# A matrix's row in three bf16 parts, and the output's residual added by VectorE, in a two-block gated decoder

## What is computed

```python
x = x + tanh(g_xattn[0]) * L0_xattn(layernorm(x), ctx, ctx)   # 16 heads, top 90% of the keys kept
x = x + tanh(g_ffn[0])   * L0_ffn(layernorm(x))               # FP4 blocks of 16, 256 -> 704 -> 256
x = x + tanh(g_xattn[1]) * L1_xattn(ctx, layernorm(x))        # layer_norm(att + decoder_seq)
x = x + tanh(g_ffn[1])   * L1_ffn(layernorm(x))               # int8 per token, 256 -> 256
# L1_xattn has no softmax: kv = einsum('bthd,bthe->bhde', k, v); att = einsum('bqhd,bhde->bqhe', q, kv) / 4
# shapes: x, ctx (8, 512, 256) f32
```

## Time and profile before

| | us |
|---|---|
| median of 3 runs | 1346.02 (1345.36 to 1349.61) |
| the profiled execution, its own time | 1342.49 |
| its span, first to last instruction | 1340.8 |
| PE busy, all stages | 1079.4 (81%) |
| DVE busy | 1037.0 (77%) |
| ACT busy | 878.0 (65%) |
| POOL busy | 95.0 (7%) |
| mean granted clock of PE, of full speed | 0.936 |

### The profile page before, as it was taken

How to read it: one execution, slowest core, us unless ns; L and a number is a source line. 1 busy time by engine, 2 the same in 40 slices (tenths; PEclk the granted TensorE clock), 3 DMA queues, 4 the chain that set the end, 5 groups by cost and what they waited for, 6 DMA issues and landing times.

```text
span 1340.8 us, 17609 instructions
## 1 busy us (share of the span) xinstructions
PE 1079.4 (81%) x5736; PEld 514.1 (38%) x5736; DVE 1037.0 (77%) x2097; ACT 878.0 (65%) x1912; POOL 95.0 (7%) x75
## 2 busy tenths in 40 slices
PE   3999994777777677777767775888999999999986
PEld 3667673011111111111111111236666666666663
DVE  3765673798888888888888884447988888888865
ACT  2232322778999999999999993664455545554543
POOL 0010023000000000000000000001111110101012
PEclk8999997557999999999999997788999999999998
DMA  7444432011221121112222201101111111110000
GB/s 229 142 165 154 149 131 64 15 32 33 42 41 33 38 41 36 27 36 39 41 41 41 41 18 47 38 9 47 52 36 37 63 44 36 36 63 28 20 21 32
DMA packets 77776, 74.89 MB, mean 56 GB/s; under 512 B 13682, under 2 KB 71284, under 8 KB 77684
## 3 DMA queue, kind: packets, MB, share of 16 engines
q1 hardware_dynamic: 77684, 73.76, 20.2%
HBM read 44.90 MB, written 28.31 MB: 55 GB/s over the span
## 4 chain that ended last, share of the span: by engine, by line
PE 36%; ACT 33%; issue 7%; DVE 5%; SPq 1%; DMA 1%; POOL 0%; ACTq 0%; DVEq 0%
ACT ea L1061 19%; ACT prob L1069 13%; PE ps_a L1275 12%; PE ps_b L1234 6%; PE ps_c L1234 4%; PE ps_v L1234 2%; PE ps_a L1255 2%; PE ps_c L918 2%; DVE nmax L962 2%; PE ps_a L1284 2%; PE ps_v L1341 1%; PE ps_c L1367 1%; PE ps_b L1330 1%; PE ps_v L933 1%; PE ps_b L891 1%
## 5 line engine op out<-in xcount | busy, mean ns | idle before, releaser
L1061 ACT ACTIVATE ea<-ps_a,nmax 128x512 f32<-128x512 f32 x512 | 361.3, 744 | 31.9 <-DVE nmax L962 31.8
L962 DVE TENSOR_REDUCE nmax<-ps_a 128x2 f32<-128x1024 f32 x256 | 312.8, 1223 | 70.0 <-PE ps_a L891 68.5
L1069 ACT ACTIVATE prob<-ps_b 128x1024 f32<-128x1024 f32 x256 | 278.2, 1087 | 46.2 <-PE ps_b L891 46.2
L891 PE MATMUL ps_b<-q_st,k_st 52*128 52x512 f16 x512 | 102.2, 395 | 143.1 <-ACT prob L1069 139.5
L891 PEld LDWEIGHTS ps_b<-q_st,k_st 52*128 52x128 f16 x512 | 25.1, 93 | 368.8 <-ACT prob L1069 337.1
L1275 PE MATMUL ps_a<-wgu,xT 128*128 128x352 f32 x512 | 164.0, 465 | 2.4 <-ACT xT L1400 2.4
L918 PE MATMUL ps_c<-ea,rz 128*32 128x512 f32 x1024 | 153.7, 676 | 1.1 <-DVE rank L1005 1.1
L933 PE MATMUL ps_v<-prob,v_in 128*16 128x512 f32 x1024 | 137.2, 608 | 11.7 <-DVE att L1029 11.5
L1061 ACT ACTIVATION_READ_ACCUMULATOR ea<-ps_a,nmax 128x1 f32 x512 | 134.4, 262 | 0.0
L891 PE MATMUL ps_a<-k_st,q_st 48*128 48x512 f16 x512 | 108.0, 419 | 31.2 <-ACT ea L1061 18.4
L1275 PEld LDWEIGHTS ps_a<-wgu,xT 128*128 128x128 f32 x512 | 94.3, 191 | 49.4 <-issue 3.9
(11 more groups left out here) (233 smaller groups left out, 1614.7 us busy)
## 6 DMA issues: line engine op xcount, KB each, us to landing
q_scr<-q_p SPq DMA_DIRECT2D x24, 256.0 KB, 2.5
k_scr<-k_p SPq DMA_DIRECT2D x24, 256.0 KB, 2.5
q_st<-q_scr SPq DMA_DIRECT2D x32, 192.0 KB, 4.6
k_st<-k_scr SPq DMA_DIRECT2D x32, 192.0 KB, 4.8
mat<-m_scr SPq DMA_DIRECT2D x16, 384.0 KB, 3.0
x_in<-in_x SPq DMA_DIRECT2D x8, 512.0 KB, 5.6
c_in<-in_ctx SPq DMA_DIRECT2D x8, 512.0 KB, 4.1
v_scr<-v_s SPq DMA_DIRECT2D x8, 512.0 KB, 2.6
```

The source lines that it names most:

```text
L891: return e.matmul(bank, left[b][o:o + rows, r, t * P:t * P + P], right[b][o:o + rows, r], start=True, stop=True)
L962: e.tensor_reduce(nmax[u % 2][:, t].rearrange("p (h r) -> p r h", h=2)[:, r], ps_a[:, z % 2 * 2:z % 2 * 2 + 2], AX_X, ALU.max, negate=True ...
L1061: e.activation(ea[c % RING][:, g % 4], ps_a[:, g % 4], ACT.Exp, bias=nmax[u % 2][:, t, n:n + 1], accum_out=tot[u % 2][:, t, n:n + 1]).then ...
L1069: e.activation(prob[g % RING][:, 2 * (z % 2):2 * (z % 2) + 2], ps_b[:, :, :], ACT.Exp).then_inc(s_prob, 1)
```

## The change

1. The row of the second attention's matrix is kept apart from the matrix. DVE writes it to one partition (`r_s`), GpSimd takes it into three bf16 parts whose sum it is (`row_parts`: three casts and two subtractions of 1x256 for each batch, each waiting for the one before), SP stores them with a DMA of its own to `scr.r`, and in `feed` a second small DMA loads them as 3 x 256 bf16. The fp32 matmul with K=1 becomes a bf16 matmul with K=3.
2. `o_b` is written by DVE as `w_ps + r4` (new `output(u)`), not by ACT as a copy. The identity matmul of `r4` is left out on PE. `output` stands behind `x_round`; in the turns 17 to 20, in which no unit enters, it is one turn later, behind `q8` of the next unit.
3. ACT's `z` stands one `leave` earlier.
4. GpSimd's and DVE's work for `rs_a` is left out in turn 20, for `rs_b` in turns 19 and 20; nobody reads those values.
5. In `project`, GpSimd's `split` is cut in three calls. `split(0)` stands ahead of the first `row_parts`, `split(1)` and `split(2)` behind the seventh.

```diff
@@ project, sync @@
                 e.dma_start(scr.m[b], m_s[b % 2][:, :]).then_inc(s_out_m[b % 2], 16)
+                e.wait_ge(s_pool_r, b + 1)
+                e.dma_start(scr.r[b].unsqueeze(0), r_p[b % 2][:, :, :]).then_inc(s_out_m[b % 2], 16)
@@ project, vector: matrix_m @@
                 if b >= 2:
-                    e.wait_ge(s_out_m[p], 16 * (b // 2))
-                e.tensor_scalar(m_s[p][:, DC * D:], psE[:, 1, 0:D], mean[p][:, DC:], None, ALU.add).then_inc(s_dve_m, 1)
+                    e.wait_ge(s_out_m[p], 32 * (b // 2))
+                if b >= 2:
+                    e.wait_ge(s_pool_r, b - 1)
+                e.tensor_scalar(r_s[p][:, 0], psE[0:1, 1, 0:D], mean[p][0:1, DC:], None, ALU.add).then_inc(s_dve_m, 1)
@@ project, gpsimd @@
-            fp4.split(e)
+            po = Tally(s_pool)
+
+            def row_parts(b):
+
+                x, y = r_s[b % 2], r_p[b % 2]
+                e.wait_ge(s_dve_m, b + 1)
+                if b >= 2:
+                    e.wait_ge(s_out_m[b % 2], 32 * (b // 2))
+                for n in range(2):
+                    e.tensor_copy(y[:, n], x[:, n]).then_inc(*po.up())
+                    e.wait_ge(*po.now())
+                    e.tensor_tensor(x[:, n + 1], x[:, n], y[:, n], ALU.subtract).then_inc(*po.up())
+                    e.wait_ge(*po.now())
+                e.tensor_copy(y[:, 2], x[:, 2]).then_inc(s_pool_r, 1)
+
+            fp4.clear(e)
+            fp4.split(e, 0)
+            for b in range(B - 1):
+                row_parts(b)
+            for k in range(1, 3):
+                fp4.split(e, k)
+            row_parts(B - 1)
@@ feed, sync: turn @@
                 e.dma_start(mat[u1 % 2][:, :], scr.m[u1 // 2]).then_inc(s_ldm[u1 % 2], 16)
+                e.dma_start(mat_row[u1 % 2][:, :], scr.r[u1 // 2]).then_inc(s_ldm[u1 % 2], 16)
@@ feed, gpsimd @@
-        for i in range(TURNS):
+        for i in range(TURNS_A):
...
-            e.wait_ge(s_ve_b, i + 1)
-            e.tensor_tensor(rs_b[p][:, :, :], ve_b[p][:, :, :], half[:, :, :], ALU.pow).then_inc(s_rs_b, 1)
+            if i < TURNS_B:
+                e.wait_ge(s_ve_b, i + 1)
+                e.tensor_tensor(rs_b[p][:, :, :], ve_b[p][:, :, :], half[:, :, :], ALU.pow).then_inc(s_rs_b, 1)
@@ feed, tensor: turn @@
-                e.matmul(y_ps.rearrange("p (n d) -> p n d", n=N), one_row[:, :],
-                         mat[p][0:1, DC * D:].unsqueeze(1).to_broadcast([1, N, D]), start=True, stop=False)
+                e.matmul(y_ps.rearrange("p (n d) -> p n d", n=N), ones16[0:3, :],
+                         mat_row[p][:, :].unsqueeze(1).to_broadcast([3, N, D]), start=True, stop=False)
...
                 e.wait_ge(s_dve_r1, min(i + 2, UNITS))
-                e.wait_ge(s_act_out, u4)
-                e.matmul(w_ps, ident[:, :], flat(r4[u4 % 3][:, :, :]), start=True, stop=False)
-                bias_row(w_ps, 1)
+                e.wait_ge(s_dve_out, u4)
+                bias_row(w_ps, 1, first=True)
@@ feed, scalar: turn @@
-            if u5 is not None:
-                e.wait_ge(s_pe_last, u5 + 1)
...
-                e.activation(flat(o_b[u5 % 2][:, :, :]), w_ps, ACT.Copy).then_inc(s_act_out, 1)
             if u0 is not None:
                 x_T(u0)
-                for q in range(4):
+                for q in range(3):
                     leave(u0, q)
...
             if u0 is not None:
+                leave(u0, 3)
                 leave(u0, 4)
@@ feed, vector @@
+        def output(u):
+            e.wait_ge(s_pe_last, u + 1)
+            if u >= 2:
+                e.wait_ge(s_sto[u % 2], 16 * (u // 2))
+            e.tensor_tensor(flat(o_b[u % 2][:, :, :]), w_ps, flat(r4[u % 3][:, :, :]), ALU.add).then_inc(s_dve_out, 1)
+
         def turn(i):
...
                 ins.then_inc(s_dve_q, 1)
+                if i > UNITS:
+                    output(u5 - 1)
+                if u5 == UNITS - 1:
+                    output(u5)
...
             if u0 is not None:
                 x_round(u0)
-            variances_b(i)
+            if u0 is not None and u5 is not None:
+                output(u5)
+            if i < TURNS_B:
+                variances_b(i)
```

More of the change, by code:

```diff
@@ L354, in round, with clear, split @@
         e.tensor_tensor(q, q, mag, ALU.add).then_inc(self.s_round, 1)
[L356 to L357 removed]
+    def clear(self, e):
         for n in (FC - 1, 2 * FC - 1):
             e.memset(self.gn[:, n], 0.0).then_inc(self.s_zero, 1)
[L360 to L368 removed]
+    def split(self, e, k):
+        po = self.pool
+        _, y, n, nb = self.third(k)
+        q, mag, grid = self.temps(k, nb)
+        e.wait_ge(self.s_round, k + 1)
+        if k:
+            e.wait_ge(self.s_split, k)
+        e.tensor_tensor(grid, q, mag, ALU.subtract).then_inc(*po.up())
+        e.wait_ge(*po.now())
+        e.tensor_tensor(y, grid, spread(self.sc[:, n:n + nb], nb), ALU.mult).then_inc(self.s_split, 1)
     def free(self, e, n):
@@ L451, in project @@
         s_dve_mean = m.sem("dve_mean")
+        s_pool, s_pool_r = m.sem("proj_pool"), m.sem("pool_r")
         s_act_ln, s_act_rs = m.sem("act_ln"), m.sem("act_rs")
```

62 lines of the change are left out of this document (27 added, 35 removed).

## The result

The changed kernel takes 1330.61 us (median of five runs, 1329.81 to 1333.29), the kernel before 1346.02 in the same session: a ratio of 0.9884, with a 95% interval of 0.9868 to 0.9901. Run once more later it took 1330.72, a ratio of 0.9886 (0.9869 to 0.9902). The forecast was 1328.0 with a range of 1321 to 1336: the sign and the size are right, the centre 2.6 us too low. The profiled run of the changed kernel is the slowest of its five (1333.29, span 1331.6), and the profiled execution of the kernel before (1342.49) is faster than any of its five timed ones, so the two traces alone are only 9.2 us apart.

What follows compares the result with a forecast made beforehand. PE sets the turn of `feed`, 27.10 us, forecast to become 25.41. `feed` gains 21.3 us and `project` loses 3.6: -17.7, so 1328.3 against the median of 1346.02, predicted as 1328; range of 8 in 10: 1321 to 1336.

Steps and rivals of the forecast that it cites:

- The bf16 row at 0.22: PE in `feed`: a bf16 row takes 0.22 us instead of the fp32 row's 1.06, saving 0.84 a turn.
- DVE's round, 25.0 to 25.1: DVE in `feed`: its round without idle time, `output` added, is 25.0 to 25.1 us, some 0.3 below PE's turn.
- Turns 4 to 14: `feed`: turn 4 gains 1.80 us, turns 5 to 14 gain 1.69 each, 16.9.
- Turn 15 and the last ones: End of `feed`: turn 15 gains 1.80 us; turns 16 and 17 gain the row's 0.84 once.
- The unread refinements, 0 to 0.24: Last int8 rounding in `feed`: leaving out the roots ahead of it gives 0.24 us at most, counted as 0.
- The end of `project`, +2.6: `split(1)` and `split(2)` behind batch 6's row parts end at 216.6, delaying PE's weight transposes 2.6 us (+1.0 to +5.0).
- DVE in the roundings, +1.0: `project`: row parts slow DVE's `round(1)` and `round(2)`, PE losing 0.9 and 0.4; 0.3 returns from `kvs`: +1.0 us.
- my second rival: `project`: every row part in both roundings takes its full length from DVE; `project` loses 6.5 us, time 1331; chance 0.09.
- DVE as the bound: `feed`: a hand-over or lost overlap costs DVE 0.8 us more, turn 25.9, time about 1334; chance 0.14.
- GpSimd hidden: `project`: row parts at 1.5 us and no blocking, `project` loses 0.7, time 1325; chance 0.09.
- Slower than before: `project`: one batch's row parts take over 22 us and eat the 21.3 gained; chance 0.04 with anything else slower.
- The row that gets no cheaper: `feed`: what follows the row waits for `decT` anyhow; 0.84 a turn lost, time 1340; chance 0.04 with other partial gains.

Runs made afterwards that it cites:

- the two halves: Each against the kernel before: the matrix row in bf16 parts alone, 1338.66 us; all the rest of the change without that row, 1336.89 us.
- the two added instructions: The changed kernel with two more 128x512 additions on DVE, read by nothing, behind `output` in turns 5 to 15: 1338.82 us.
- the runs with parts of 10.2 us: 16 more casts in each batch's row parts: in the changed kernel 1337.89 us; with `split(1)`, `split(2)` ahead of row parts of batches 4, 5, 1331.84.
- the later kernels: The changed kernel with `split(1)`, `split(2)` ahead of row parts of batches 5, 6: 1327.34 us; 4, 5: 1326.53; that with a `kvs(5)` wait: 1324.65, again 1327.50.

## Why the prediction was right, step by step

- **PE sets the turn.** Right. PE is busy for all but 0.39 us, and the two halves alone gave 26.37 and 26.25, against 26.35 and 26.25 worked out from the same rows.
- **The bf16 row at 0.22.** Mis-sized. Its pitch is 0.31 (1092.53 to 1092.84), so it saves 0.75 and not 0.84. That is the whole difference between 25.41 and 25.51. The price was taken from a bias row, whose neighbours are others. PE's weight loads (PEld in the timeline of the same turn) show the difference:

```profile
1092.84 1.59 PEld L1265 LDWEIGHTS ps_v<-mat,decT 128*128 128x128 f32 x8 [0.23 <-issue]
...
1101.41 1.71 PEld L1265 LDWEIGHTS ps_c<-w,q8T 128*128 128x128 f32 x8
```

Behind the bias row the next product's load starts together with the row (1101.41), behind the new row it starts 0.31 later, with the product itself. The kernel before has the same, 1099.76 behind its bias row and 1090.22 behind the fp32 row of 1089.17, so it could have been read there. Why the load comes later is not shown.
- **The identity matmul, -0.96, and output on DVE, +0.11.** Right: 26.25 from 27.10 in the half that holds only these, and a gap of 0.39 where I had said about 0.4.
- **DVE's round, 25.0 to 25.1.** Right: 24.97 by the idle time, 24.9 by the two added instructions. "About 2 us ahead of `o_b`" in the list of signs was wrong, and contradicts this step: a round of 25.0 in a turn of 25.5 leaves 0.5, and 0.54 is there. The 2 us would have been those of the first such turn only (0.99 there).
- **Turns 2 and 3 gain nothing.** Right. Turn 3 takes 23.32 us, before 23.35, and `x_T` at its end stood for `xg` in PE's timeline:

```profile
976.31 0.66 PE L1286 MATMUL ps_a<-ident,xg 128*128 128x128 f32 x4 [0.63 <-DVE xg L1621]
```

- **Turns 4 to 14.** 1.80 and ten of 1.69, 18.7, were forecast; 1.69 and ten of 1.59, 17.6, came. The term that was off is the row's pitch alone.
- **Turn 15 and the last ones.** Wrong. 2.64 forecast, 1.3 came, and all of the 1.3 is the unread refinements (next point): with them put back the stretch takes 76.5 us as before. Up to the first transposes of the last hidden values, where I had 1.80, the trace shows 0.36 (29.81 to 29.45). The row gives 0.73 there (29.08 in the kernel with it alone). The identity matmul of turn 15 stands behind the down product in PE's order, off the chain, so its 0.96 should not have been counted. And `z` ahead of the fourth `leave` costs 0.4 in that turn. Behind it the 0.36 is lost again (46.7 us before, 47.1 with the refinements back), and the 0.84 of turns 16 and 17 doesn't show. PE's granted clock is lower in this stretch, 0.86 against 0.91 from `x_T` of turn 15 to the end, and the last but one group of eight products takes 3.61 us instead of 2.00. The sum had no term for the clock; how much of the loss is the clock's was not measured by itself.
- **The unread refinements, 0 to 0.24.** Mis-sized: 1.3 us by the trace. I had read what stands between ACT's `n4` and the last rounding in the kernel before. That is 0.24. But in the new order `output` of the unit before, 0.6 us, stands ahead of them on the same engine, so they end 0.84 after `n4` does. I had named that 0.6 and used it as a reason to count nothing, where it pushes the roots onto the chain. And DVE's leftovers outlast the store for 0.6 more.
- **GpSimd's parts, 3.1 us a batch.** Right: 2.85 us (93.42 to 96.27), with 0.39 to 0.46 for a cast and 0.66 for a subtraction.
- **The end of `project`, +2.6.** The path was right, a stretch was missing. GpSimd's last third was forecast for 216.6, which is 146.6 after batch 0's store, and ended at 146.5. What I missed is that DVE's `m_mean` is held until then, so that 1.04 us of `r_s`, `m_s` and the hand-over come behind it and not beside it: 3.5 in the profiled pair, 1.7 against a `project` whose clock falls.
- **DVE in the roundings, +1.0.** Wrong: nothing in sum. The two engines did meet, and GpSimd paid (timeline of all engines, changed kernel; the row parts are batch 4's, beside `round(1)` at the start of batch 6):

```profile
160.56 2.25 POOL L771 CAST r_p<-r_s 1x256 bf16<-1x256 f32 x1 [19.45 <-DVE r_s L668]
...
160.81 1.74 DVE L349 TENSOR_TENSOR fq<-gn,fs 128x1536 f32<-128x1536 f32 x1
...
162.59 1.04 DVE L351 TENSOR_SCALAR fm<-fq 128x1536 uint32<-128x1536 uint32 x1
...
162.89 1.25 POOL L773 TENSOR_TENSOR r_s<-r_s,r_p 1x256 f32<-1x256 f32 x1
...
163.66 1.30 DVE L353 TENSOR_SCALAR fm<-fm 128x1536 f32<-128x1536 f32 x1
...
164.21 1.01 POOL L771 CAST r_p<-r_s 1x256 bf16<-1x256 f32 x1
...
165.00 1.83 DVE L355 TENSOR_TENSOR fq<-fq,fm 128x1536 f32<-128x1536 f32 x1
...
165.30 2.06 POOL L773 TENSOR_TENSOR r_s<-r_s,r_p 1x256 f32<-1x256 f32 x1
...
167.54 0.41 DVE L639 SCALAR_TENSOR_TENSOR rb<-rows,psE 128x256 f32<-128x256 f32 x1
```

The parts took 7.25 us here instead of 2.85; the rounding's four instructions took 1.74, 1.04, 1.30 and 1.83 instead of 1.75, 0.96, 0.96 and 1.76, so 0.5 us together, inside the room of 0.58 that the earlier trace rows showed. PE's next product (L532, now L538) was on time, 6.98 us after the start of its `gram` products in both traces. `round(2)` looks the same (DVE 1.60, 0.98, 1.24 and 1.70 us instead of 1.61, 0.89, 0.89 and 1.62). The 0.3 that I gave back for the free `kvs` came: from batch 4's store to batch 5's it is 22.24 us instead of 22.48. But batches 3 and 4 each come 0.1 later in every kernel with row parts, for a reason that isn't traced, so batch 6's store stands 133.2 us after batch 0's in both traces. (The `kvs` rows of 0.42 and 1.53 us in the earlier trace rows are those of batches 6 and 5; I had called them 7 and 6.) The Trainium skill, "SBUF — State Buffer", section "Who interferes with whom", has the second to issue wait for the first. `kvs` behind GpSimd's long multiplication agrees (1.53 us, ending 0.27 after it); `m_mean`, which has one input in SBUF, was held too (1.13 us, ending 0.01 after GpSimd's). The roundings don't agree: GpSimd's first cast starts at 160.56, ahead of DVE's `fq` at 160.81, and yet `fq` takes its usual 1.74 us and the cast 2.25 instead of 0.46. Taken as a price for DVE, as in my second rival, the rule would have cost 3.9 in the two roundings; the trace has 0.5 us more work on DVE in each and no time lost.
- **SP, 0.** Right for parts of 2.85 us (`c_in` issued at 86.7, read at about 97), and the runs with parts of 10.2 us show the price beyond it: PE stood 0.93 us for a load in batch 1.

**The rivals.** DVE as the bound (1334) didn't come, by 0.5 us a turn, and the run with 1.46 us more shows what it would look like. GpSimd in DVE's way (1331.2) is nearer to the measured time than the forecast, for the wrong reason: nothing in the roundings, all at the end. GpSimd hidden (1325) is what the order of the later kernels nearly reaches, 1324.7 to 1327.5. Slower than before needed 22 us a batch; 10.2 cost 7 us. The row that gets no cheaper fell with the half that has it alone, 7.5 us less than before.

By its own steps the forecast promised 1.1 too much in the steady turns and 1.3 in the last ones, and its two terms for `project` missed in opposite directions: 3.6 forecast, 3.5 by the trace. -17.7 becomes -15.4, and 1346.0 less that is 1330.6. That `project` came out right is luck: two terms missed and cancelled. The agreement to a tenth is luck too: the 3.5 is from a kernel before whose clock stayed up, with 1.7 the sum would be -17.2, and the interval of the measured ratio allows 13.3 to 17.8 us. What the prediction had right for its own reason is the steady turns, 17.6 of 18.7.

## What to carry to other kernels

Once the pitch of a turn is known to be one engine's, compare the new turn with every other engine's round, its idle time taken out; the difference is all that will be left of their idle time, wherever it stood. Look at who is held when a slow engine's long instruction is moved: here it was not only the engine that waits for it by a semaphore, but a tiny instruction of DVE that was issued into it, with a chain of its own behind. Take the price of an instruction from a row with the same neighbours, the weight loads included. And before a microsecond is explained from two traces, look at the granted clock of the stretch in both, and at a third trace in which the stretch is unchanged.
